# Decoder on one core: values and denominators of the first self-attention by one product

## What is computed

```
qkv = (x @ W_qkv).reshape(Bx, Nx, 3, H, Dh).transpose(2, 0, 3, 1, 4)
allowed = jnp.abs(i - j) <= half
attn = jnp.einsum('bhqd,bhkd->bhqk', q, k) * scale
attn = jnp.where(allowed[None, None], attn, -jnp.inf)
attn = jax.nn.softmax(attn, axis=-1)
out = jnp.einsum('bhqk,bhkd->bhqd', attn, v)
x = x + out.reshape(Bx, Nx, C) @ W_proj + b_proj        # x normalised first
```

## Time and profile before

| | |
|---|---|
| median of three runs | 1504.77 us (1500.16 to 1508.09) |
| profiled execution | 1504.03 us, span 1502.4 us |
| TensorE granted clock, mean | 0.993 |
| TensorE, VectorE, ScalarE, GpSimd busy in the span | 95%, 50%, 41%, 33% |
| first self-attention, one batch in the steady part | 24.77 us |

### The profile page before, as it was taken

One profiled execution on the slowest core, in us unless ns is written; L12 is line 12 of the kernel. 1 busy time (PEld: TensorE's weight loads), 2 busy tenths in 40 slices (PEclk: granted clock), 3 DMA queues, 4 the chain that ended last, 5 costly groups with the idle time before them and its releaser, 6 DMA issues. The chain is left out here.

```text
span 1502.4 us, 34667 instructions
## 1 busy us (share of the span) xinstructions
PE 1433.9 (95%) x11880; PEld 1159.7 (77%) x11881; DVE 748.7 (50%) x2160; ACT 619.1 (41%) x1711; POOL 490.5 (33%) x758
## 2 busy tenths in 40 slices
PE   7999998988999999999999999999899899999998
PEld 5676766767899999976777777777666579999997
DVE  6666757887433333344444444444278862222222
ACT  2433346653222222235445444545366533333332
POOL 3545442444322122223233233333224452222222
PEclk9999999999999999999999999999999999999999
DMA  9920000152243434120000000000001522533332
GB/s 316 333 69 2 2 2 9 45 176 62 50 119 67 144 71 114 32 64 1 0 1 1 1 1 1 1 1 0 1 16 44 174 78 40 149 93 94 94 90 34
DMA packets 79666, 97.46 MB, mean 65 GB/s; under 512 B 10523, under 2 KB 72579, under 8 KB 79555
## 3 DMA queue, kind: packets, MB, share of 16 engines
q1 hardware_dynamic: 64643, 77.58, 16.4%
q0 software_dynamic: 13680, 17.19, 6.6%
q10 hardware_dynamic: 1232, 1.18, 0.2%
HBM read 57.51 MB, written 39.59 MB: 65 GB/s over the span
## 5 line engine op out<-in xcount | busy, mean ns | idle before, releaser
L1741 POOL TENSOR_TENSOR L1a_prob<-L1a_prob,L1a_rtot 128x1024 f32<-128x1024 f32 x64 | 121.1, 1892 | 275.8 <-DVE L1a_rtot L1614 275.8
L2270 PEld LDWEIGHTS L0x_ps<-L0f_rows_t,L0f_w_up 128*128 128x128 f32 x1584 | 183.7, 193 | 10.4 <-issue 9.0
L2270 PE MATMUL L0x_ps<-L0f_rows_t,L0f_w_up 128*128 128x128 f32 x1584 | 185.8, 277 | 5.6 <-issue 4.8
L2346 ACT ACTIVATE L1f_hid<-L1x_ps,L1f_b_up 128x128 f32<-128x128 f32 x296 | 92.4, 363 | 163.0 <-PE L1x_ps L2270 159.7
L2270 PEld LDWEIGHTS L1x_ps<-L1f_rows_t,L1f_w_up 128*128 128x128 f32 x1184 | 139.5, 194 | 3.4 <-issue 1.6
L2270 PE MATMUL L1x_ps<-L1f_rows_t,L1f_w_up 128*128 128x128 f32 x1184 | 140.4, 277 | 0.6 <-ACT L1f_rows_t L2330 0.6
L2279 PE MATMUL L1x_ps<-L1f_w_down,L1f_hid 128*128 128x256 f32 x592 | 134.1, 380 | 1.9 <-issue 1.9
L2214 POOL TENSOR_TENSOR turn<-eps 128x1 f32<-128x1 f32 x74 | 13.6, 184 | 372.3 <-DVE wv L2448 367.7
L1683 ACT ACTIVATE L1a_prob<-L1a_ps_s,L1a_nmax 128x256 f32<-128x256 f32 x256 | 118.2, 473 | 38.1 <-DVE L1a_nmax L1609 38.1
L2279 PEld LDWEIGHTS L1x_ps<-L1f_w_down,L1f_hid 128*128 128x128 f32 x592 | 109.6, 190 | 15.5 <-issue 2.1
L1245 POOL TENSOR_SCALAR_AFFINE_SELECT L0a_prob<-L0a_prob 128x128 f32<-128x128 f32 (+1 forms) x256 | 79.8, 353 | 104.3 <-ACT L0a_prob L1199 104.3
(11 more groups left out here) (486 smaller groups left out, 2812.5 us busy)
## 6 DMA issues: line engine op xcount, KB each, us to landing
expert_table<-zero SPq DMA_DIRECT2D x1, 16640.0 KB, 68.5
L0f_w_up<-in_w_dram SPq DMA_DIRECT2D x8, 1408.0 KB, 6.8
L1f_w_up<-in_w_dram SPq DMA_DIRECT2D x8, 1024.0 KB
L1f_w_down<-in_w_dram SPq DMA_DIRECT2D x8, 1024.0 KB
L0f_w_down<-in_w_dram SPq DMA_DIRECT2D x8, 768.0 KB, 8.7
L1f_rows<-expert_table SPq DMA_DIRECT2D x35, 130.0 KB
L0f_rows<-expert_table SPq DMA_DIRECT2D x32, 130.0 KB
sums<-X SPq DMA_DIRECT2D x8, 256.0 KB
```

Source lines behind the costliest of these rows:

```text
L1741: eng.tensor_tensor(v, v, r.unsqueeze(2).to_broadcast([P, 2 * QT_N, S]), ALU.mult).then_inc(norm_done, 1)
L2270: ins = eng.matmul(ps_h[c][:, o:o + P], w_up[par][:, t, w0:w0 + P], rows_t[:, t, :], start=(t == 0), stop=(t == DT - 1))
L2346: ins = eng.activation(hid[:, c, k * P:(k + 1) * P], ps_h[c][:, k * P:(k + 1) * P], ACT.Gelu, bias=b_up[par][:, 2 * c + k:2 * c + k + 1])
```

## The change

One product now gives values and denominators. `v_s` is filled with 1.0 once, and each head's 16 values go to the even ones of its 32 columns. As weights, 32 columns are taken: for an even head from its first on, for an odd head one column earlier, so that values come out in even rows and sums in odd rows, or the other way round. Even and odd unit of a chunk write the left and the right half of `ps_o`. When both are done ScalarE copies the bank to SBUF (`gather`), and four transfers that ScalarE issues (`move`) bring the sums of both heads of a pair into equal rows of `summed`, and the values into those of `valued`. VectorE's reciprocal and product then read these two. The rows of the output projection's weights are laid out in the new order on the host (`in_turn`). The last two units (`direct`) keep the old way; for them half of a value tile is set back to 0.

The sums and the product of a chunk move from the odd unit behind it to the even unit after that: behind the maxima in unit 0, ahead of them in unit 2. The keys are so copied ahead of the sums. The output projection goes from MID to END of unit 2.

```diff
-    MID = [[], [(1, "k")], [(-1, "o")], []]
-    END = [[(1, "q")], [], [], [(2, "x")]]
+    MID = [[], [(1, "k")], [], []]
+    END = [[(1, "q")], [], [(-1, "o")], [(2, "x")]]
...
+        def weights_of(i, t, head):
+            columns = v_s[i][:, t, :, :].rearrange("p h n -> p (h n)")
+            return columns[:, 2 * DH * head - head % 2:2 * DH * (head + 1) - head % 2]
+        def direct(u):
+            return u >= units - 2
...
                 def sums(b, c):
-                    eng.wait_ge(values_done, 2 * (b * 2 + c + 1))
-                    eng.reciprocal(rsum[:, :], ps_o[:, S:2 * S]).then_inc(rsum_done, 1)
+                    n = b * 2 + c
+                    if n:
+                        eng.wait_ge(o_out, n)
...
+                        eng.wait_ge(sums_moved, 32 * (n + 1))
+                        eng.reciprocal(rsum[:, :], summed_t[:, :]).then_inc(rsum_done, 1)
...
                 for u in range(units):
                     b, c, v = part(u)
-                    whole = part(u - 2)[:2] if v == 1 and u > 1 else None
-                    if whole:
-                        sums(*whole)
+                    whole = part(u - 4)[:2] if v == 0 and u >= UNITS else part(u - 2)[:2] if u == units - 1 else None
...
                     shift(u)
-                    if whole:
+                    if whole and u % UNITS:
+                        sums(*whole)
                         out(*whole)
                     if u + 1 < units:
                         for r in range(GROUPS):
                             maximum(u + 1, r)
-                    for e in of(MID, u):
+                    if whole and u % UNITS == 0:
+                        sums(*whole)
+                        out(*whole)
...
+                def gather(n):
+                    eng.wait_ge(values_done, 2 * (n + 1))
+                    if n:
+                        eng.wait_ge(sums_moved, 32 * n)
+                        eng.wait_ge(values_moved, 32 * n)
+                    eng.activation(both[:, :, :], ps_o[:, :].rearrange("p (w s) -> p w s", w=2), ACT.Copy).then_inc(copied, 1)
+                def move(n):
+                    eng.wait_ge(copied, n + 1)
+                    if n:
+                        eng.wait_ge(o_out, n)
+                    for w in range(2):
+                        eng.dma_start(summed_t[w::2, :], both[1 - w::2, w, :]).then_inc(sums_moved, 16)
+                    for w in range(2):
+                        eng.dma_start(valued_t[w::2, :], both[w::2, w, :]).then_inc(values_moved, 16)
...
+                    if u % 2 == 1 and u > 1:
+                        move(u // 2 - 1)
                     for r in range(GROUPS):
                         exponential(u, r)
+                    if u % 2 == 0 and u:
+                        gather(u // 2 - 1)
...
-                            eng.wait_ge(o_out, u // 2)
-                    for summed in range(2):
+                            eng.wait_ge(copied, u // 2)
+                    for summed in range(2 if direct(u) else 1):
```

More of the change, by code:

```diff
@@ L1005, in attention_banded @@
         rsum, o_t = sb("rsum", [P, S]), sb("o_t", [P, 2, S])
+        both, summed_t, valued_t = sb("both", [P, 2, S]), sb("summed", [P, S]), sb("valued", [P, S])
         built, cleared, tops_cleared = sem("built"), sem("cleared"), sem("tops_cleared")
@@ L1013, in attention_banded @@
         values_done, rsum_done, o_out = sem("values"), sem("rsum"), sem("o_out")
+        copied, sums_moved, values_moved = sem("copied"), sem("sums_moved"), sem("values_moved")
         projected, added, biased = sem("projected"), sem("added"), sem("biased")
@@ L1044, in wait_free @@
                 eng.wait_ge(exp_done, u * GROUPS + r + 1)
-        def odd_even(v):
-            return v.rearrange("p (a two) (half d) -> p a (two half) d", two=2, half=2)[:, :, 0::3, :]
+        def weights_of(i, t, head):
[3 more added lines that the diff above has]
+            return u >= units - 2
         with nc.Block() as block:
@@ L1064, in _ @@
                     eng.wait_ge(built, 4 * v + 3)
-                    eng.memset(ones[:, v, v * DH:(v + 1) * DH], 1.0).then_inc(built, 1)
+                    eng.memset(ones[:, v, v::2], 1.0).then_inc(built, 1)
                 eng.memset(none[:, :], 0.0).then_inc(built, 1)
@@ L1095, in take @@
                         ins.then_inc(out_vector, 1)
-                    elif e == "o":
+                    if e == "o":
                         eng.wait_ge(projected, b + 1)
@@ L1116, in sums @@
                 def sums(b, c):
-                    eng.wait_ge(values_done, 2 * (b * 2 + c + 1))
-                    eng.reciprocal(rsum[:, :], ps_o[:, S:2 * S]).then_inc(rsum_done, 1)
+                    n = b * 2 + c
+                    if n:
+                        eng.wait_ge(o_out, n)
+                    if direct(2 * n):
+                        eng.wait_ge(values_done, 2 * (n + 1))
+                        eng.reciprocal(rsum[:, :], ps_o[:, S:2 * S]).then_inc(rsum_done, 1)
+                    else:
+                        eng.wait_ge(sums_moved, 32 * (n + 1))
+                        eng.reciprocal(rsum[:, :], summed_t[:, :]).then_inc(rsum_done, 1)
                 def out(b, c):
-                    eng.wait_ge(rsum_done, b * 2 + c + 1)
+                    n = b * 2 + c
+                    eng.wait_ge(rsum_done, n + 1)
                     if c == 0 and b:
                         eng.wait_ge(projected, b)
-                    eng.tensor_tensor(o_t[:, c, :], ps_o[:, 0:S], rsum[:, :], ALU.mult).then_inc(o_out, 1)
+                    if not direct(2 * n):
+                        eng.wait_ge(values_moved, 32 * (n + 1))
+                    eng.tensor_tensor(o_t[:, c, :], ps_o[:, 0:S] if direct(2 * n) else valued_t[:, :], rsum[:, :], ALU.mult).then_inc(o_out, 1)
                 norm(0, 0)
@@ L1130, in _ @@
                 for i in range(2):
-                    eng.memset(v_s[i][:, :, :, :], 0.0).then_inc(cleared, 1)
+                    eng.memset(v_s[i][:, :, :, :], 1.0).then_inc(cleared, 1)
                 norm(1, 0)
@@ L1155, in _ @@
                             maximum(u + 1, r)
-                    for e in of(MID, u):
+                    if whole and u % UNITS == 0:
+                        sums(*whole)
+                        out(*whole)
+                    if u == units - 6:
+                        eng.wait_ge(values_done, u - 1)
+                        eng.memset(v_s[(B - 1) % 2][:, :, HEADS // 2:HEADS, :], 0.0).then_inc(cleared, 1)
+                    for e in of(MID, u) + of(END, u):
                         take(*e)
@@ L1188, in take @@
                     else:
-                        eng.wait_ge(cleared, 2)
+                        eng.wait_ge(cleared, 3 if b == B - 1 else 2)
                         for t in range(KT):
-                            ins = eng.activation(odd_even(v_s[b % 2][:, t, :, :]), src[:, t, :].rearrange("p (a two d) -> p a two d", two=2, d=DH),
-                                                 ACT.Copy)
+                            ins = eng.activation(v_s[b % 2][:, t, :, 0::2], src[:, t, :].rearrange("p (h d) -> p h d", d=DH), ACT.Copy)
                     ins.then_inc(out_scalar, 1)
@@ L1341, in values @@
                         if u:
-                            eng.wait_ge(o_out, u // 2)
-                    for summed in range(2):
+                            eng.wait_ge(copied, u // 2)
+                    for summed in range(2 if direct(u) else 1):
                         for t in range(KT):
                             for r in range(GROUPS):
[L1346 to L1349, removed]
+                                o = (summed if direct(u) else v) * S + first_key[t]
+                                lhs = ones[:, v, :] if summed else weights_of(b % 2, t, c * 8 + 2 * r + v)
+                                ins = eng.matmul(ps_o[rows(r), o:o + W], lhs, prob[u % 2][:, r, t, :],
+                                                 start=(t == 0 and (v == 0 and not summed if direct(u) else True)),
+                                                 stop=(t == KT - 1 and (v == 1 or not direct(u))), skip_group_check=True)
                     ins.then_inc(values_done, 1)
@@ L2719, with in_turn @@
     down0[:, 0:full + GATED_TAIL] = i["L0_ffn_W3"].transpose(0, 2, 1)
+    def in_turn(w):
+        return w.reshape(-1, 2, 16, *w.shape[1:]).swapaxes(1, 2).reshape(w.shape)
     laid = {
@@ L2723 @@
         "wq0": qkv[:, 0:256], "wk0": qkv[:, 256:512], "wv0": qkv[:, 512:768],
-        "wo0": i["L0_attn_W_proj"], "bo0": i["L0_attn_b_proj"],
+        "wo0": in_turn(i["L0_attn_W_proj"]), "bo0": i["L0_attn_b_proj"],
         "wq1": i["L0_xattn_wq"].T, "wk1": i["L0_xattn_wk"].T, "wv1": i["L0_xattn_wv"].T, "wo1": i["L0_xattn_wo"].T,
```

## The result

The change makes the kernel slower: 1520.02 us, the median of three runs (1519.01 to 1521.33), against 1504.77; the ratio is 1.0105, its 95% interval 1.006 to 1.015. The forecast was 1510, within a range of 1495 to 1523. The direction of the sum was right and its size was not: 5 us were forecast and 15 came. The forecast's own range, 1501 to 1517, does not hold the result; the stated one does only because its upper end was taken from late transfers, which did not come. That is luck.

What follows compares the result with a forecast made beforehand. TensorE was taken to bound the first self-attention at the full clock. From 1504.0 us, -1.25 for the first batch, +4.5 for five rounds, +0.7 and +1.9 at the end gave 1509.9, rounded to 1510; range 1495 to 1523.

Steps and rivals of the forecast that it cites:

- The forecast's own range: Total time of 1501 to 1517 us, with a round between 24.3 and 26.4; given a chance of 0.62.
- late transfers: Rival: the sums' transfers land slowly and seven units 2 wait 1.7 to 2 us more, +13, 1523 us; chance 0.14.
- The ones leave: TensorE loses 0.76 us of ones products in 30 of 32 units: 3.06 a round, 22.9 us at most.
- The last projection later, the sums before the maxima: In unit 2 TensorE waits 2.2 us more for maxima behind the reciprocal; this half round is 1.94 us longer.
- the lower end, 0.42: Fastest time in us allowed for VectorE's reciprocal reading SBUF, equal to the shift's for as many elements.
- the first wait for GpSimd: In unit 2, TensorE waits some 1 us ahead of unit 1's values, hidden under the wait for VectorE's maxima.
- The other half of the round: From the value projection's end on, GpSimd's wait loses 0.5 us of the gain; the whole round becomes 25.67, +0.9.
- Copy, transfers and other edits: ScalarE's added copy (0.60 us) and four issues (0.49 each) per chunk hidden or 0.3; transfers land in 2.2.
- the point of decision: Landing time of the sums' transfers, 4.2 us, past which they would make unit 2 wait.
- held issues: Rival: ScalarE's first four issues are held behind SyncE's bulk loads until about 80 us, +40, 1550 us; chance 0.07.
- Beginning and end: First batch -1.25 us; last key projection to unit 29's second scores +0.7; from there to the final projection +1.9.
- the full gain: Rival: VectorE's chain is shorter than thought, so the removed ones products pay fully; 1490 us; chance 0.17.

Runs made afterwards that it cites:

- before_no_ones: The kernel before the change with the products with the ones left out, so denominators are missing; 1485.13 us, ratio 0.9899.
- short_reciprocal: The changed kernel with VectorE's reciprocal taking 16 of 256 columns from the second chunk on, order kept; 1499.90 us, ratio 0.9972 to the kernel before.
- filled: The changed kernel with eight idle identity products in unit 2 ahead of the second scores, from the second batch on; 1508.66 us, ratio 1.0046 to the kernel before.
- no_transfers: The changed kernel without each chunk's four transfers, reciprocal and product reading the copy directly; 1516.8 us, ratio 1.0108 to the kernel before.
- sums_behind: The changed kernel with sums and product behind the maxima in unit 2, output projection left at that unit's end; 1525.65 us, ratio 1.0132 to the kernel before.
- o_unit3: The changed kernel with sums and product behind the maxima in unit 2 and the output projection at unit 3's end; 1492.34 us, ratio 0.9943 to the kernel before.

## Why the prediction was right in its mechanism and short in its size

- **The ones leave**: right. Alone they are worth 1.0% (before_no_ones), with 2.06 of 3.06 us kept in a round.
- **The last projection later, the sums before the maxima**: right to 0.04 us. The second scores of unit 2 start at 7.46 (7.42 forecast), the reciprocal from SBUF takes 1.74 (1.76 taken; the lower end, 0.42, was far off), and the first wait for GpSimd lies under the second. short_reciprocal shows the chain to be the cause.
- **What I then made of that wait is the step that failed**: "TensorE stands 2.2 us more", and behind it "second scores 0.86 to 8.28, projection 1.82". Both durations were taken from rows at the full clock, though the step before them had just put a wait of 2.2 us there. From 20 us to the final projection the trace of before has no wait on TensorE over 0.84. They measured 1.20 and 3.13, and a steady round 27.3, outside the 24.3 to 26.4 that I had given it. Six such places at 1.6 are 9.6 of the 10.1 us by which the stretches behind the first exceed their forecast; filled takes 0.6 of the 1.05% away by filling the wait with work.
- **The other half of the round**: right. Values of unit 3 wait for GpSimd (0.23 in the bracket); the round at the full clock is 25.70 (25.67 forecast).
- **Copy, transfers and other edits**: right. ScalarE's issues took 0.47 to 1.57 us each, also beside the zero fill, and were hidden. That transfers land in 2.2 was wrong beside the bulk loads: it was 5.5, past the 4.2 that I gave as the point of decision; it did no harm because the issues begin 2.7 us earlier than I had placed them, beside the copies ahead of them. The Trainium skill, "DMA: Bandwidth & Descriptors", section Queues, rings and completion order, has DMA engines take turns between rows of rings by the packet. That ScalarE's row moved at all beside a full SyncE row agrees; a delay of 3.6 us for 64 KB is more than the one packet's that I had made of it. The same section says that the two issuing engines have no descriptor generator of their own, so by it held issues were not without a chance, as I had written; the 0.47 to 1.57 us refute them.
- **Beginning and end**: first batch -1.22 (-1.25 forecast). Second scores of unit 25 to those of unit 29 +2.5 against +0.7, and the last stretch +3.7 against +1.9; 1.6 of each is once more the clock, already among the six places.
- **Rivals**: late transfers and held issues are refuted by the trace and by no_transfers, and the full gain by the chain. The kernel is slower by more than 0.5%. Of the 0.31 that I gave that, 0.21 stood on these two, which did not come, and 0.10 on the forecast's own mechanism, whose range ended at 1517; the clock stood in none of it.

## What to carry to other kernels

When a schedule worked out from a trace puts a wait on TensorE that the trace does not have, the products behind the wait must be priced at both levels of its clock, not only at that of the rows. Work that is taken off an engine also takes away cover: ask of each semaphore wait, a PSUM ring's above all, what now stands ahead of it on the releasing engine. A projection or another block without haste belongs behind the point at which its input is certain to be there, so that it covers someone else's latency and adds no wait of its own.

## What the runs showed of the hardware

After about 2 us in which TensorE did next to nothing (0.12 us of work in 2.00), the granted clock stood at half for some 3.4 us (0.58 and 0.56 over 4 us), and products took up to 1.7 times as long (a four-product projection 3.13 against 1.82). After the first such wait of the same length (57.9) it did not fall, and in no_transfers 6.8 us at half came with a shorter one (1.89), so the length of a wait alone does not tell. Nor is the fall tied to one place: in the changed kernel it came about 0.5 us behind the end of the wait (110.88), in sums_behind 1.3 behind it (59.43), with TensorE at work again, and in no_transfers inside the wait, 0.9 ahead of its end. Waits of up to 1.02 (short_reciprocal) and 1.05 (o_unit3) never cost it between 20 us and the stage's end. Eight idle products in the wait kept the clock full in every round. A transfer of 64 KB within SBUF landed in 1.9 us when the DMA engines were free and in 5.5 (median) in the first 100 us, most of it beside DMA engines that moved 344 GB/s in all. Its issue on ScalarE was delayed little, 0.47 to 1.57 against 0.47 to 0.62 from 100 us on, though SyncE's own next issue behind the fill took 57.63.
